# Deformable sampling by whole tiles: VectorE in 12 operations in place of 27, exponentials and sums on ScalarE

## The chip, the cores and the metric

The kernel runs on one core of a Trainium2 chip. The metric is the device time of one execution in microseconds (us). The engines are TensorE (PE in the rows, its weight loads PEld), VectorE (DVE), ScalarE (ACT), GpSimd (POOL) and SyncE (SP), the last of which here only issues DMAs.

## The reference

The program is a stack of layers. The part that matters is layer 0, a deformable attention over 4 images of 64 x 64 pixels with 128 channels in 4 groups of 32. For each pixel and group it takes 9 taps at positions that a small network gives, and each tap is a bilinear mix of 4 corner cells:

```python
out = gather(y0, x0) * (1 - wy_) * (1 - wx_) + gather(y0, x0 + 1) * (1 - wy_) * wx_ + gather(y0 + 1, x0) * wy_ * (1 - wx_) + gather(y0 + 1, x0 + 1) * wy_ * wx_
return out * mask[:, None]
...
attn = jax.nn.softmax(jnp.einsum('bgnc,bgckn->bgnk', qf, ks_), axis=-1)
out = jnp.einsum('bgnk,bgckn->bgnc', attn, vs_)
...
return out @ w_proj + b_proj
```

So every pixel has 36 taps (4 groups of 9), each with 4 corners, of keys and of values; scores against the query, a softmax over the 9 taps of a group, and a weighted sum. Layer 1 is a linear attention over the same tokens; layers 2 and 3 follow it.

## The kernel before

Layers 0 and 1 are one function, `first_layers`. For each image b, `points(b)` computes convolutions, offsets and weights, and writes a table of records (one record holds the 4 corners' keys and values of a cell, 256 floats) and a table `meta` with one row of 308 floats a pixel (36 indices, 144 corner weights, the query). Then the sampling loop goes over 128 tiles of 128 pixels (32 tiles an image). `linear(b)` is layer 1.

The sampling loop is software-pipelined by hand. GpSimd issues 36 indirect DMAs a tile (line 511), one per tap, each of which gathers 128 records of 1 KB into `rec`. `rec` is a ring of 4 half tiles (18 taps each), so two tiles fit. VectorE works a tile in two halves h = 0, 1. A half is: multiply keys by query (L1051), reduce to dots (L1052), weight (L1053), sum corners (L1054), maximum (L1055), subtract (L1056); wait for ScalarE's exponential (L780); sum (L1062), reciprocal (L1063), share (L1064), corner weights (L1066), multiply values (L1068), reduce into `att_t` (L1070). L1049 copies the query into PSUM ahead of a tile. Each of these goes through `Chain`, which makes the next VectorE instruction wait for the semaphore `s_dve` of the one before. `scored(t, h)`, `summed(t, h)` and `added(t)` are values that `s_dve` has reached at these points. GpSimd may gather half h of tile t+2 when `summed(t, h)` is reached.

After a tile TensorE turns `att_t` (L678), ScalarE copies it out of PSUM (`turned`, L769), TensorE projects (`project`, L668), VectorE adds residual and bias (`add`, L1030 and L1031, in the second half of the next tile), and ScalarE stores (`store`, L773).

The work of `points(1..3)` (47 slots each) and `linear(0..2)` (38 slots each) is spread over the same loop: the generator `sides` hands out 2 slots a tile, in the order points 1, points 2, linear 0, points 3, linear 1, linear 2, on every engine at a place of its own in the code. TensorE's side work are "jobs": a group of matmuls into one of 4 PSUM banks `ps`, which ScalarE copies out (L706 for the qkv jobs of `points`, L758 for the qv jobs of `linear`, others alike). Job n waits until the copy of job n-4 is made. ScalarE copies a slot's jobs one slot later (qkv jobs in the same slot). The longest side work of VectorE is the depthwise filter: 24 slots of `points(b)` with 9 operations each (L840, L842).

## Time and profile before

| what | value |
|---|---|
| time, median of 3 runs | 9669.89 us (9655.2 to 9689.33) |
| profiled execution: span | 9686.6 us |
| VectorE busy | 6067.7 us, 8431 instructions |
| GpSimd busy | 4575.1 us, 4608 of its instructions are gathers |
| TensorE busy | 3083.5 us |
| ScalarE busy | 1385.9 us |
| first and last gather start | 216.8 us, 6828.6 us |
| last reduce of the sampling loop ends | 6883 us |

The profiled execution's span, 9686.6 us, is its whole time; it is 0.2% above the median of the runs. Sampling, with the side work beside it, takes the stretch from 217 to 6883 us. The remaining 2804 us are layers that the change doesn't touch.

How to read the times of TensorE: a matmul's row tells when it was issued and an end that is modelled; when its result was there is seen at the engine that waited for it.

### The profile page before, as it was taken

What the parts mean: (1) busy time and instruction counts of PE and PEld (TensorE: products, weight loads), DVE (VectorE), ACT (ScalarE), POOL (GpSimd) and SP (SyncE); (2) the same over time, 40 slices, a digit from 0 to 9 for tenths busy, and PEclk for the clock granted to TensorE, in tenths of its full rate; (3) what the DMA queues carried; (4) which work ended last, traced back from release to release, by engine and by line L of the source; (5) the groups of instructions that cost most, each with busy time, mean ns of one, the idle gap of its engine ahead of it and who ended that gap; (6) DMA issues with size and microseconds to landing.
All of it is one profiled execution on the core that took longest, in us unless ns stands there. A gap on an engine that the chain in (4) does not pass through costs nothing. (4 is left out here: it accounts for less than half of the span.)

```text
span 9686.6 us, 108210 instructions
## 1 busy us (share of the span) xinstructions
PE 3083.5 (32%) x41476; PEld 2213.2 (23%) x41476; DVE 6067.7 (63%) x8431; ACT 1385.9 (14%) x2582; POOL 4575.1 (47%) x4747
## 2 busy tenths in 40 slices
PE   4102101021001101021001100101255476999997
PEld 2001000010001000010001000100233365788885
DVE  6567675776775557685875557545673565555554
ACT  1000000000000000000000000000122232444442
POOL 0766666666677567666777667766100000000000
PEclk7555555565555555555555555555677788999998
DMA  4434345343353234343453234323123443222224
GB/s 86 121 93 111 95 111 145 95 111 92 109 155 99 80 94 126 90 114 91 111 155 99 86 97 121 102 88 96 38 45 127 110 105 90 60 66 67 66 66 179
DMA packets 822930, 966.58 MB, mean 100 GB/s; under 512 B 283028, under 2 KB 643560, under 8 KB 817896
## 3 DMA queue, kind: packets, MB, share of 16 engines
q0 software_dynamic: 221184, 604.27, 21.1%
q1 hardware_dynamic: 573880, 321.25, 13.4%
q10 hardware_dynamic: 27440, 34.87, 1.0%
q8 instruction: 328, 5.37, 0.2%
q14 instruction: 98, 0.80, 0.0%
HBM read 797.64 MB, written 155.99 MB: 98 GB/s over the span
## 5 line engine op out<-in xcount | busy, mean ns | idle before, releaser
L511 POOL DMA_INDIRECT l_rec<-records,l_row x4608 | 4518.7, 981 | 2309.6 <-issue 1421.4
L1070 DVE TENSOR_REDUCE l_att_t<-l_rec 128x64 f32<-128x2304 f32 x256 | 1025.5, 4006 | 8.8
L2323 DVE COPY l3p_mix<-l3p_ps 128x512 f32<-128x512 f32 x1024 | 659.9, 686 | 576.1 <-PE l3p_ps L2199 576.1
L668 PE MATMUL l_pso<-l_wo,l_att_c 128*128 128x128 f32 x256 | 101.9, 501 | 2560.9 <-issue 1684.5
L1051 DVE TENSOR_TENSOR l_rec<-l_rec,l_psv 128x2304 f32<-128x2304 f32 x256 | 653.7, 2553 | 202.5 <-DMA l_rec<-records,l_row 88.7
L678 PE MATMUL l_pso<-l_id,l_att_t 128*128 128x128 f32 x128 | 58.0, 453 | 2114.1 <-DVE l_att_t L1070 1472.7
L1068 DVE TENSOR_TENSOR l_rec<-l_rec,l_psv 128x2304 f32<-128x2304 f32 x256 | 653.7, 2554 | 100.6 <-DVE l_psv L1066 67.8
L780 ACT ACTIVATE l_prob<-l_score 128x18 f32<-128x18 f32 x256 | 56.1, 219 | 4381.0 <-DVE l_score L1056 1442.2
L1052 DVE TENSOR_REDUCE l_psv<-l_rec 128x72 f32<-128x2304 f32 x256 | 655.6, 2561 | 11.4 <-remote 1.7
L668 PEld LDWEIGHTS l_pso<-l_wo,l_att_c 128*128 128x128 f32 x256 | 64.2, 312 | 2607.0 <-issue 1717.9
L2285 ACT ACTIVATE l3p_mix<-l3p_ps 128x512 f32<-128x512 f32 x1024 | 557.7, 597 | 662.8 <-PE l3p_ps L2199 662.8
L2199 PE MATMUL l3p_ps<-l3p_psi,l3p_ms 32*128 32x128 f32 x16384 | 611.6, 283 | 21.3 <-DVE l3p_mix L2323 16.8
L2160 POOL COPY l3p_four<-l3p_fil 128x128 f32 (+1 forms) x64 | 18.8, 294 | 1197.0 <-PE l3p_psm L2252 1196.1
L2199 PEld LDWEIGHTS l3p_ps<-l3p_psi,l3p_ms 32*128 32x128 f32 x16384 | 519.4, 186 | 180.5 <-ACT l3p_mix L2285 108.7
L678 PEld LDWEIGHTS l_pso<-l_id,l_att_t 128*128 128x128 f32 x128 | 23.7, 185 | 2166.6 <-DVE l_att_t L1070 1506.8
L1062 DVE TENSOR_REDUCE l_psv<-l_prob 128x2 f32<-128x18 f32 x256 | 46.0, 180 | 572.0 <-issue 297.7
L842 DVE SCALAR_TENSOR_TENSOR l_psc<-l_area,l_wd,l_psc 128x512 f32<-128x512 f32 x504 | 381.0, 756 | 24.7 <-DVE l_psc L842 6.2
L2149 POOL MEMSET l3p_xs<- 128x4096 f32 x1 | 3.5, 3512 | 800.9 <-POOLq L55 800.9
L1030 DVE TENSOR_TENSOR l_done<-l_pso,l_res 128x128 f32<-128x128 f32 x128 | 37.4, 292 | 485.2 <-remote 354.5
L1514 POOL MEMSET l2b_res<- 128x512 f32 x1 | 0.5, 525 | 595.2 <-POOLq L55 595.2
L2216 PE MATMUL l3p_psy<-l3p_mix,l_mats 128*32 128x128 f32 x8192 | 259.6, 273 | 1.0 <-ACT l3p_yr L2294 0.8
L2216 PE MATMUL l3p_psy<-l3p_mix,l3p_xs 128*32 128x128 f32 x8192 | 258.9, 273 | 0.0
(359 smaller groups left out, 6394.6 us busy)
## 6 DMA issues: line engine op xcount, KB each, us to landing
l_rec<-records,l_row POOLq DMA_INDIRECT x4608
l2b_w<-l_w SPq DMA_DIRECT2D x32, 1024.0 KB, 10.9
records<-l_area SPq DMA_DIRECT2D x48, 512.0 KB
l_row<-meta SPq DMA_DIRECT2D x124, 154.0 KB
l_x_hat<-l3a_xout ACTq DMA_DIRECT2D x32, 512.0 KB, 4.6
l3p_xin<-l_x_hat SPq DMA_DIRECT2D x128, 128.0 KB, 3.1
l_y_raw<-l3p_yr SPq DMA_DIRECT2D x64, 256.0 KB, 3.4
l3p_yin<-l_y_raw SPq DMA_DIRECT2D x128, 128.0 KB, 2.9
```

The source lines that it names most:

```text
L511: pool.indirect_dma_start(out=rec[:, r, k, :], out_offset=None, in_=records[b].rearrange("r c d -> r (c d)"), in_offset=bass.IndirectOffse ...
L668: pe.matmul(ps_p, att_c[:, :], wo0_s[:, :], start=True, stop=True).then_inc(s_proj, 1)
L678: pe.transpose(ps_a, att_t[t % 2][:, :], id_s[:, :]).then_inc(s_att, 1)
L842: step_a(dve.scalar_tensor_tensor(acc if t < TAPS - 1 else to, window(f, g, t), wd_s[:, f, t:t + 1], acc, ALU.mult, ALU.add))
L1051: step(dve.tensor_tensor(keys, keys, asked.broadcast_to([P, HG, TAPS * CORNERS, HC]), ALU.mult))
L1052: step(dve.tensor_reduce(flat, rec[:, r, :, :].rearrange("p k (c d) -> p (k c) d", c=CORNERS)[:, :, 0:HC], AX, ALU.add))
L1068: step(dve.tensor_tensor(values, values, ps_w.rearrange("p (g m) -> p g m", g=HG).unsqueeze(3).broadcast_to([P, HG, TAPS * CORNERS, HC]), ...
L1070: step(dve.tensor_reduce(att_t[two][:, HG * HC * h:HG * HC * (h + 1)].rearrange("p (g d) -> p g d", g=HG), values.rearrange("p g m d -> p ...
L2199: mm = pe.matmul(bank.rearrange("p (x c e) -> p x c e", x=2, e=2)[:, i // 2, :, i % 2], ms[32 * g:32 * g + 32, 4 * q + i, :], psi[s][32 * ...
L2216: mm = pe.matmul(ps_y[32 * g:32 * g + 32, c, :], flat[:, 32 * m - 8 * r:32 * m - 8 * r + 32], mix[s][:, :, 2 * m + kind, :], start=r == 0 ...
L2285: act.activation(mix[t.side(0)][:, x:x + 2, :, :].rearrange("p x c e -> p (x c e)"), ps[(2 * q + h) % 3][:, 0, :], ACT.Copy).then_inc(s_se ...
L2323: dve.tensor_copy(mix[t.side(0)][:, x:x + 2, :, :].rearrange("p x c e -> p (x c e)"), ps[(2 * q + h) % 3][:, 1, :]).then_inc(s_setd, 1)
```

## The change

A tile is worked on whole. `Chain` steps on VectorE go from 27 a tile to 12: the two halves are joined, the query's copy goes to ScalarE (`ask`), the maximum and subtraction become one minimum (the query is now scaled by a negative factor, and ScalarE's exponential takes `scale=-1.0` and the minimum as `bias`), and the sums come from `accum_out` of 4 exponentials, one a group (`weigh`). GpSimd's gathers of tile t+2 now wait once, for all of tile t (`summed(t)`). On TensorE and ScalarE the loop is written in another order.

```diff
-            def half(b, s, h):
-                r = 2 * (s % 2) + h
-                for k in range(HT):
-                    c = HT * h + k
...
+            def gather(b, s):
+                for c in range(GT):
+                    r = 2 * (s % 2) + c // HT
...
-                for h in range(2):
-                    if s >= 2:
-                        pool.wait_ge(s_dve, summed(s - 2, h))
-                    half(0, s, h)
+                if s >= 2:
+                    pool.wait_ge(s_dve, summed(s - 2))
+                gather(0, s)
...
             for t in range(TILES):
-                if t:
-                    project(t - 1)
+                pe.wait_ge(s_dve, summed(t))
+                pe.transpose(ps_a, att_t[t % 2][:, :], id_s[:, :]).then_inc(s_att, 1)
+                project(t)
                 next(side)
                 next(side)
-                pe.wait_ge(s_dve, summed(t, 1))
-                pe.transpose(ps_a, att_t[t % 2][:, :], id_s[:, :]).then_inc(s_att, 1)
-            project(TILES - 1)
...
+            def ask(t):
+                act.wait_ge(s_row[t % AHEAD], 16 * (t // AHEAD + 1))
+                return act.activation(ps_q, row[t % AHEAD][:, QUERY:META], ACT.Copy)
+
+            def weigh(t):
+                act.wait_ge(s_dve, scored(t))
+                for g in range(GROUPS):
+                    k = slice(TAPS * g, TAPS * g + TAPS)
+                    ins = act.activation(prob[:, k], score[:, k], ACT.Exp, bias=low[:, g:g + 1], scale=-1.0, accum_out=total[:, g:g + 1])
+                if t + 1 < TILES:
+                    ins = ask(t + 1)
+                ins.then_inc(s_exp, 1)
...
             for t in range(TILES):
-                for h in range(2):
-                    act.wait_ge(s_dve, scored(t, h))
-                    act.activation(prob[:, :], score[:, :], ACT.Exp).then_inc(s_exp, 1)
-                    if h == 0 and t >= 1:
-                        turned(t - 1)
-                    if h == 0 and t >= 2:
-                        store(t - 2)
-                    next(side)
+                weigh(t)
+                if t >= 1:
+                    store(t - 1)
+                turned(t)
+                next(side)
+                next(side)
...
                 for h in range(2):
-                    r = 2 * two + h
...
+                    dve.wait_ge(s_rec[2 * two + h], 16 * HT * (t // 2 + 1))
+                step(dve.tensor_tensor(keys, keys, asked.broadcast_to([P, GROUPS, TAPS * CORNERS, HC]), ALU.mult))
+                step(dve.tensor_reduce(flat, held.rearrange("p k (c d) -> p (k c) d", c=CORNERS)[:, :, 0:HC], AX, ALU.add))
+                step(dve.tensor_tensor(flat, flat, wgt, ALU.mult))
+                step(dve.tensor_reduce(score[:, :], dots[:, :, :], AX, ALU.add))
+                dve.tensor_reduce(low[:, :], score[:, :].rearrange("p (g k) -> p g k", k=TAPS), AX, ALU.min).then_inc(s_dve, 1)
...
+                if t >= 1:
+                    add(t - 1, step)
...
+                dve.wait_ge(s_exp, t + 1)
+                step(dve.reciprocal(inverse, total[:, :]))
...
-                    next(side)
+                next(side)
+                next(side)
```

ScalarE's order, at the qv jobs of `linear(0)`, before. `l_prob` is the exponential of a half tile, `l_att_c` is `turned`, `x<-l_done` the store, L758 the copies of qv jobs.

```order
L780 ACTIVATE l_prob<-l_score 128x18 [waits l01_dve]
L769 ACTIVATE l_att_c<-l_pso 128x128 [waits l01_att]
L773 DMA x<-l_done 128x128 [waits l01_dve]
L758 ACTIVATE l_area<-l_ps 128x512 [waits l01_l_job] x3
L780 ACTIVATE l_prob<-l_score 128x18 [waits l01_dve]
L758 ACTIVATE l_area<-l_ps 128x512 [waits l01_l_job] x3
```

And the same place after the change:

```order
L772 ACTIVATE l_prob,l_total<-l_score,l_low 128x9 [waits l01_dve]
L772 ACTIVATE l_prob,l_total<-l_score,l_low 128x9 x3
L766 ACTIVATE l_psv<-l_row 128x128 [waits l01_row3]
L783 DMA x<-l_done 128x128 [waits l01_dve]
L779 ACTIVATE l_att_c<-l_pso 128x128 [waits l01_att]
L755 ACTIVATE l_area<-l_ps 128x512 [waits l01_l_job] x6
```

Before, a tile's two exponentials stand 3 copies apart, and its turned result is that of the tile before; now a tile has all its exponentials in one place, and 6 copies and its own `turned` stand between them and the next tile's.

GpSimd's order in the loop before (the wait on `l01_dve` is the one for `summed`):

```order
L511 DMA l_rec<-records,l_row 128x256 [waits l01_dve,l01_row2]
L511 DMA l_rec<-records,l_row 128x256 x17
L511 DMA l_rec<-records,l_row 128x256 [waits l01_dve]
L511 DMA l_rec<-records,l_row 128x256 x17
L511 DMA l_rec<-records,l_row 128x256 [waits l01_dve,l01_row3]
```

And after:

```order
L512 DMA l_rec<-records,l_row 128x256 [waits l01_dve,l01_row2]
L512 DMA l_rec<-records,l_row 128x256 x35
L512 DMA l_rec<-records,l_row 128x256 [waits l01_dve,l01_row3]
L512 DMA l_rec<-records,l_row 128x256 x35
```

The second wait within a tile is gone, and the first now stands for a whole tile.

## Rows read from the trace of the kernel before

**Rows 1.** The page: span; busy us, share, instructions of engines.

```profile
span 9686.6 us, 108210 instructions
PE 3083.5 (32%) x41476; PEld 2213.2 (23%) x41476; DVE 6067.7 (63%) x8431; ACT 1385.9 (14%) x2582; POOL 4575.1 (47%) x4747
```

**Rows 2.** Stretches: us, busy PE, PEld, DVE, ACT, POOL; clock, DMA share, GB/s.

```profile
217.00:6883.00 6666.00, 843.29 (x2254) 470.72 (x2254) 4365.83 (x4755) 349.65 (x812) 4518.46 (x4608) 0.53 0.38 107
217.00:1487.00 1270.00, 175.94 (x382) 78.02 (x382) 868.56 (x933) 61.28 (x149) 883.29 (x904) 0.53 0.39 109
...
2696.00:3696.00 1000.00, 109.86 (x369) 80.45 (x369) 595.36 (x661) 54.80 (x122) 682.94 (x684) 0.53 0.37 106
3696.00:4917.00 1221.00, 174.19 (x385) 78.33 (x385) 870.03 (x937) 61.31 (x150) 826.54 (x860) 0.53 0.38 107
...
5911.00:6883.00 972.00, 108.90 (x370) 80.22 (x370) 595.93 (x661) 55.58 (x122) 640.53 (x642) 0.52 0.34 98
```

**Rows 3.** Line 511, the gathers: what ended the idle time before them.

```profile
L511 POOL DMA_INDIRECT l_rec<-records,l_row x4608: 943/949/5119, 216.8 to 6828.6; - x192
...
  DVE l_att_t L1070: 552.1, 74
...
  DVE l_psv L1049: 119.0, 7
```

**Rows 4.** VectorE's groups from 217 to 6883 us: busy, mean ns | idle before.

```profile
L1070 DVE TENSOR_REDUCE l_att_t<-l_rec 128x64 f32<-128x2304 f32 x256 | 1025.5, 4006 | 8.8
L1052 DVE TENSOR_REDUCE l_psv<-l_rec 128x72 f32<-128x2304 f32 x256 | 655.6, 2561 | 11.4 <-remote 1.7 <-issue 0.9
L1068 DVE TENSOR_TENSOR l_rec<-l_rec,l_psv 128x2304 f32<-128x2304 f32 x256 | 653.7, 2554 | 100.6 <-DVE l_psv L1066 67.8 <-issue 22.2 <-remote 5.6
L1051 DVE TENSOR_TENSOR l_rec<-l_rec,l_psv 128x2304 f32<-128x2304 f32 x256 | 653.7, 2553 | 202.5 <-DMA l_rec<-records,l_row 88.7 <-remote 42.6 <-issue 42.6
...
L1049 DVE COPY l_psv<-l_row 128x128 f32<-128x128 f32 x127 | 37.4, 294 | 46.9 <-remote 20.4 <-DVE l_area L842 14.0 <-issue 7.2
```

**Rows 5.** The sum over six stretches with filter slots, 36 tiles in all.

```profile
sum 1917.00, PE 270.27 PEld 131.38 DVE 1469.95 ACT 76.95 POOL 1283.24; mean PE 45.05 PEld 21.90 DVE 244.99 ACT 12.82 POOL 213.87
```

**Rows 6.** Timeline in a filter stretch: start, us, instruction [idle before].

```profile
634.27 0.18 DVE L1063 RECIPROCAL l_psv<-l_psv 128x2 f32<-128x2 f32 x1 [2.30 <-remote]
...
636.38 0.18 DVE L1064 TENSOR_TENSOR l_psv<-l_prob,l_psv 128x18 f32<-128x18 f32 x1 [1.93 <-remote]
...
638.48 2.55 DVE L1068 TENSOR_TENSOR l_rec<-l_rec,l_psv 128x2304 f32<-128x2304 f32 x1 [1.16 <-DVE l_psv L1066]
```

**Rows 7.** Timeline at the qv jobs of `linear(0)`, with gathers running.

```profile
3040.05 0.60 ACT L758 ACTIVATE l_area<-l_ps 128x512 f32<-128x512 f32 x1 [14.73 <-remote]
...
3040.70 2.08 PE L643 MATMUL l_ps<-l_wn,l_area 128*128 128x256 f32 x4 [11.50 <-issue]
...
3051.25 0.60 ACT L758 ACTIVATE l_area<-l_ps 128x512 f32<-128x512 f32 x1 [10.60 <-remote]
...
3062.45 0.60 ACT L758 ACTIVATE l_area<-l_ps 128x512 f32<-128x512 f32 x1 [10.60 <-remote]
3062.95 0.21 ACT L780 ACTIVATE l_prob<-l_score 128x18 f32<-128x18 f32 x1
3063.26 0.18 DVE L1062 TENSOR_REDUCE l_psv<-l_prob 128x2 f32<-128x18 f32 x1 [15.25 <-issue]
```

**Rows 8.** Timeline at the qkv jobs of `points(2)`: gathers stop, jobs go on.

```profile
1707.68 0.69 ACT L706 ACTIVATE l_area<-l_ps,l_bn 128x512 f32<-128x512 f32 x1 [4.21 <-issue]
...
1712.58 0.69 ACT L706 ACTIVATE l_area<-l_ps,l_bn 128x512 f32<-128x512 f32 x1 [4.21 <-remote]
...
1715.39 1.85 ACT L706 ACTIVATE l_area<-l_ps,l_bn 128x512 f32<-128x512 f32 x3
...
1723.89 0.95 POOL L511 DMA_INDIRECT l_rec<-records,l_row  x1 [15.54 <-DVE l_psv L1049]
```

**Rows 9.** Line 739, an exponential with `accum_out`: ns min/median/max.

```profile
L739 ACT ACTIVATION_READ_ACCUMULATOR l_area<-l_area,l_kmax x4: 187/188/188, 2984.3 to 6932.8; 128x1 f32 x4
```

More of the change, by code:

```diff
@@ L284, in first_layers @@
         s_gate = st.gates()
-        STEPS, ADDS = 27, 2
+        STEPS, ADDS = 12, 2
         TILES = BATCH * NT
@@ L292, in cells_of, with begun, scored, summed @@
             return records[b][0:GROUPS * TH * TH, :, :].rearrange("(g y x) c d -> g y x c d", g=GROUPS, x=TH)
-        def begun(t, h):
-            return STEPS * t - ADDS * int(t >= 1) + 13 * h
-        def scored(t, h):
-            return begun(t, h) + 6 + int(h == 0)
+        def begun(t):
+            return STEPS * t - ADDS * int(t >= 1)
+        def scored(t):
+            return begun(t) + 5
         def added(t):
-            return scored(t + 1, 1) + ADDS if t + 1 < TILES else begun(TILES, 0) + ADDS
-        def summed(t, h):
-            return begun(t, h) + 12 + (1 if h == 0 else ADDS * int(t >= 1))
+            return (scored(t + 1) if t + 1 < TILES else begun(TILES)) + ADDS
+        def summed(t):
+            return begun(t + 1)
         PG, LG = 47, 38
@@ L526, in _ @@
                         hold(pool, s_row[s], 16 * i + 16, s_gate[1])
-                        for h in range(2):
-                            hold(pool, s_dve, AHEAD * STEPS * (i - 1) + summed(s + 2, h), s_gate[1])
-                            half(b, s, h)
+                        hold(pool, s_dve, AHEAD * STEPS * (i - 1) + summed(s + 2), s_gate[1])
+                        gather(b, s)
         @block.tensor
@@ L715, in points @@
                                 for t in range(AHEAD):
-                                    act.activation(row[t][:, QUERY:META], bank[:, t * P:t * P + P], ACT.Copy, scale=float(HC) ** -0.5)
+                                    act.activation(row[t][:, QUERY:META], bank[:, t * P:t * P + P], ACT.Copy, scale=-float(HC) ** -0.5)
                             if at == 0 and b in (1, 2):
@@ L776, in _ @@
             side = sides(points, linear)
+            ask(0).then_inc(s_asked, 1)
             for t in range(TILES):
-                for h in range(2):
-                    act.wait_ge(s_dve, scored(t, h))
-                    act.activation(prob[:, :], score[:, :], ACT.Exp).then_inc(s_exp, 1)
-                    if h == 0 and t >= 1:
-                        turned(t - 1)
-                    if h == 0 and t >= 2:
-                        store(t - 2)
-                    next(side)
-            turned(TILES - 1)
-            store(TILES - 2)
+                weigh(t)
[4 more added lines that the diff above has]
+                next(side)
             store(TILES - 1)
@@ L1074, in _ @@
-            step = Chain(dve, s_dve, s_gate[2], begun(TILES, 0))
+                step = Chain(dve, s_dve, s_gate[2], begun(t))
+                held = rec[:, 2 * two:2 * two + 2, :, :].rearrange("p r k d -> p (r k) d")
+                view = held.rearrange("p (g k) (c d) -> p g (k c) d", k=TAPS, c=CORNERS)
+                asked = ps_q.rearrange("p (g o d) -> p g o d", o=1, d=HC)
+                keys, values = view[:, :, :, 0:HC], view[:, :, :, HC:2 * HC]
+                wgt = row[s][:, GT:QUERY]
@@ new lines, in _ @@
+                step(dve.tensor_reduce(score[:, :], dots[:, :, :], AX, ALU.add))
+                dve.tensor_reduce(low[:, :], score[:, :].rearrange("p (g k) -> p g k", k=TAPS), AX, ALU.min).then_inc(s_dve, 1)
+                step.n += 1
+                assert step.base + step.n == scored(t)
+                if t >= 1:
+                    add(t - 1, step)
+                    assert step.base + step.n == added(t - 1)
+                dve.wait_ge(s_exp, t + 1)
+                step(dve.reciprocal(inverse, total[:, :]))
@@ new lines, in _ @@
+                step(dve.tensor_tensor(share.rearrange("p (g k) -> p g k", k=TAPS), prob[:, :].rearrange("p (g k) -> p g k", k=TAPS),
+                                       inverse.unsqueeze(2).broadcast_to([P, GROUPS, TAPS]), ALU.mult))
+                step(dve.tensor_tensor(ps_w.rearrange("p (k c) -> p k c", c=CORNERS), wgt.rearrange("p (k c) -> p k c", c=CORNERS),
+                                       share.unsqueeze(2).broadcast_to([P, GT, CORNERS]), ALU.mult))
+                step(dve.tensor_tensor(values, values, ps_w.rearrange("p (g m) -> p g m", g=GROUPS).unsqueeze(3).broadcast_to(
+                    [P, GROUPS, TAPS * CORNERS, HC]), ALU.mult))
@@ L1075, in _ @@
+                dve.tensor_reduce(att_t[two][:, :].rearrange("p (g d) -> p g d", g=GROUPS),
+                                  values.rearrange("p g m d -> p g d m"), AX, ALU.add).then_inc(s_dve, 1)
+                step.n += 1
+                assert step.base + step.n == summed(t)
+                next(side)
+                next(side)
+            step = Chain(dve, s_dve, s_gate[2], begun(TILES))
             add(TILES - 1, step)
```

66 lines of the change are left out of this document (19 added, 47 removed).

## The prediction

> **What bounds the kernel now.** I read the stretches first. Sampling with its side work lasts from 217 to 6883 us, 6666 us of the span of 9686.6 us; of this VectorE is busy 4366 us and GpSimd 4518 us [rows 1, 2]. Neither is full, so I looked for who waits for whom. The gathers come next: 4608 of them, 36 a tile, start between 216.8 and 6828.6 us; a gather takes 0.95 us and 0.30 us lie between two, so a tile costs 36 x 1.25 = 45.1 us of issue, and 128 tiles 5773 us. The waits of GpSimd for VectorE's last reduce and for its next copy are 552.1 + 119.0 = 671 us in 81 waits [rows 3]. So GpSimd is the bound for 5773 us, and about 850 us are lost to waits and slower gathers. By parts: the three stretches of `points` take 1209 to 1270 us for 23.5 tiles each (52 us a tile), the three of `linear` 972 to 1000 us for 19 tiles (52 us) [rows 2]. VectorE hardly ever waits for data: 88.7 us in all before L1051 [rows 4].
>
> What holds VectorE up is of two kinds. In filter slots its small steps cost far more than their work: 0.18 us of work stands behind gaps of 2.30, 1.93 and 1.16 us [rows 6]; six such stretches, 36 tiles, take 1917 us with 1470 us of VectorE work, 53 us a tile [rows 5]. Elsewhere TensorE's side jobs are slow: while gathers run, ScalarE's copies of qv jobs come 11.2 us apart though one job is 4 matmul and 4 weight-load instructions, 1.4 us each, and the exponential behind them in ScalarE's order comes as late as they: VectorE's sum stood idle 15.25 us for it [rows 7]. When GpSimd stands still (15.54 us), the jobs soon go fast: copies at 1707.68 and 1712.58 are 4.9 us apart, then three come within 1.85 us [rows 8]. The whole kernel thus has a self-regulating loop: gathers slow TensorE, TensorE delays the exponentials, these delay VectorE, and VectorE in the end stops the gathers.
>
> **What the change saves on VectorE.** The four large operations of a half are 4.01 + 2.56 + 2.55 + 2.55 = 11.67 us, 23.35 us a tile [rows 4]. By the copy of 128 elements in 0.294 us and the multiply of 2304 in 2.554 us, an element costs 1.04 ns and an instruction 0.16 us more, so joining two halves saves 4 x 0.16 = 0.65 us. Of 19 small operations of 0.17 to 0.29 us, about 4.0 us, 8 stay with about 2.1 us. With 0.035 us between instructions a tile goes from 28.4 to 25.2 us: 3.2 us x 128 = 410 us of VectorE time, which counts only where VectorE is last. In filter slots the exposed small steps fall from about 19 to 8, so I halve the gaps: busy 25.2 + 14.4 for two filter slots (18 operations of 0.76 us and their gaps) + 10 of gaps = 49 us against 53.
>
> The Trainium skill speaks for the change here: "VectorE: DVE Perf Modes", section on the TRN2 errata, says that an instruction on SBUF data pays a fixed latency, so that one large tile pays once and many small ones each time; its fp32 formula has 151 cycles at 0.96 GHz, by which 15 instructions fewer save an estimated 302 us in all. The rows' 0.16 us agree with it.
>
> **What it adds on ScalarE.** Four exponentials at 0.21 us, each with an accumulator read of 0.19 us [rows 7, 9], and the query's copy, 0.29 us by VectorE's copy [rows 4]: 1.9 us between `scored` and the release of VectorE, in place of two times 0.21 + 0.1. The copy was off VectorE's wait before; this is +1.3 us in VectorE's line a tile, about what the copy and the two sums saved.
>
> **What it takes away in slack.** Before, half h of tile t+2 needs half h of tile t: the buffer comes free half by half, three halves' issue after it was filled (3 x 22.6 = 67.7 us), and needs about 2 us of landing and 14 us of work: some 51 us in which VectorE may be held up before GpSimd stops. Now it must be free one tile's issue, 45.1 us, after it was filled, and needs 2 + 25 us: 18 us of slack. A hold of 40 us that GpSimd rode out before now stops it for about 20.
>
> **What it puts in VectorE's line.** This is the term that decides. After the change ScalarE's order is exponentials(t), store, turned(t), two slots of copies, exponentials(t+1), and TensorE's is turn(t), project(t), two slots of jobs. Call x the end of tile t on VectorE. TensorE starts the jobs of two slots only after turn and project, 6 instructions of 1.4 us = 8.4 us; ScalarE must copy the first slot's jobs before it gives the next exponentials. For qv, kt, vt, qt jobs that is 3 x 11.2 = 33.6 us; then 1.9 us, then the second part of VectorE's tile, 2.55 x 2 + 4.01 x 2 + three small ones = 13.7 us. Next x: 8.4 + 33.6 + 1.9 + 13.7 = **57.6 us** later. Before, the exponential of the second half stood between the two slots, and the transposes came a tile later against the side work; such tiles cost 75 us when they came in a row but VectorE and GpSimd had worked ahead, and the average over `linear` was 52.
>
> Jobs that need more than GpSimd's 45.1 us: in the qkv slots ScalarE copies all 12 jobs (12 x 5.6 = 67 us; one such job is 4 instructions), in the off4/offm slots 3 jobs of 12 instructions (50 us), in the last slots of `linear` 3 qt jobs and 2 of 16 instructions (78 us). GpSimd then stops at x + 45.1, the jobs stay slow some 5 us more [rows 8], then run fast, some 2 us: x + 52 + 1.9 + 13.7 = **68 us**.
>
> **The sum.** In one `points` of 23.5 tiles I count, by slots: 3 tiles of qkv and 3 of off4/offm at 68, 3 of offc/offs at 65, 1.5 of qt and 2 of kt/vt at 58, 6 filter tiles without jobs at 49, 5 others at 46: 408 + 195 + 203 + 294 + 230 = 1330 us, against (1270 + 1209 + 1221)/3 = 1233 with the first tile's 65 us of filling in the first one; without it 1212. That is about +118. In one `linear` of 19 tiles: 3 at 68, 8.5 at 58, 7.5 at 46: 204 + 493 + 345 = 1042, against 989 on the mean (994 is the middle one): +53. Three of each: 3 x (118 + 53) = 513; the first tile, of which VectorE now needs both halves, +7. Some tiles that I count at 68 overlap slots at a fraction, and a fast tile follows where VectorE is ahead; I take 70 us off for this: **+450 us**, 10137 us in the profile's terms and 10120 against the median, which is 0.2% lower.
>
> **Rivals.** (a) *TensorE gets quicker, the faster side* (0.20): if its instruction under gathers costs r = 0.9 in place of 1.4 us, for instance because 15 fewer semaphore steps a tile on VectorE relieve what both share, a 58 us tile is 30r + 15.6 = 43, so 46 by GpSimd (36 tiles, -432); offc/offs and off4/offm tiles come to 50 and 53 (18 tiles, -270), qkv and the last slots of `linear` to 64 and 65 (18 tiles, -63). That is -765 on the forecast, 9360 us; by a straight line between the two it breaks even at r = 1.1. For it: the jobs are fast as soon as GpSimd stands. Against it: they are slow because of the gathers, and these stay. (b) *It cancels* (0.05): the saving in filter tiles, 36 x 4 to 36 x 8 = 150 to 290 us, against loaded tiles that keep their fast followers: 9640 to 9700. (c) *The handshakes too* (0.20): in slots 3 to 5 of `points` and 7 to 9, 24, 25 of `linear` VectorE waits for TensorE's job of the same slots. Before, that job had been issued most of a tile earlier; now it starts with VectorE's slot, behind 8.4 us of turn and project. 33 such waits of 8 to 12 us with 18 us of slack: +150 to +300 on the forecast, 10300 to 10450. (d) The forecast (0.55): 9800 to 10300.
>
> The granted clock, 0.52 to 0.54 in the stretches [rows 2], is near the lower level of 1.2 GHz before and should be so after; I give it nothing.
>
> **Numbers.** A measurement can tell about 0.3%, 29 us. Slower by more: 0.55 + 0.20 = 0.75; same 0.05; faster 0.20. The range leaves 1 in 10 of the faster end and 1 in 10 of the slowest: 9620 to 10480.
>
> **What would show it.** Right: the gathers' waits for VectorE's last reduce grow from 671 to about 1100 us, in most tiles; VectorE's idle time moves to the reciprocal behind the exponentials, with ScalarE copying late jobs; copies still 11.2 and 5.6 us apart while gathers run; VectorE's work falls by about 400 us; filter tiles near 49 us. Wrong: copies of jobs much closer together under gathers (then rival a), or small steps on VectorE with no gaps, or exponentials that do not stand behind late copies.

## The result, and the profile after

The changed kernel takes 9843.85 us (median of 4 runs, 9839.98 to 9855.23), the kernel before, run beside it, 9679.61 (4 runs, 9655.2 to 9691.68): ratio 1.0169, interval 1.0153 to 1.0185, 164 us slower. The forecast was +450 with the range 9620 to 10480: the sign and the range held, the size was nearly three times too large.

The page of the changed kernel, to be read against [rows 1]:

```profile
span 9853.4 us, 106326 instructions
PE 3062.5 (31%) x41476; PEld 2212.3 (22%) x41476; DVE 5717.2 (58%) x6511; ACT 1524.3 (15%) x3478; POOL 4639.8 (47%) x4747
```

VectorE works 350 us less and GpSimd, with the same 4608 gathers, 65 us more. The stretches between the ends of the same tiles as in [rows 2], with the same columns:

```profile
217.00:1478.00 1261.00, 165.36 (x382) 74.73 (x382) 801.80 (x573) 87.56 (x316) 883.25 (x891) 0.54 0.39 108
1478.00:2711.00 1233.00, 172.06 (x377) 75.16 (x376) 778.16 (x564) 85.71 (x307) 828.01 (x838) 0.53 0.40 109
2711.00:3745.00 1034.00, 103.65 (x373) 78.30 (x373) 534.56 (x373) 76.15 (x257) 688.95 (x684) 0.52 0.37 103
3745.00:4960.00 1215.00, 167.24 (x385) 75.93 (x385) 811.21 (x578) 87.72 (x317) 845.29 (x855) 0.54 0.39 107
4960.00:6004.00 1044.00, 102.28 (x369) 75.53 (x368) 545.02 (x375) 76.10 (x256) 690.79 (x687) 0.52 0.37 104
6004.00:7034.00 1030.00, 99.86 (x369) 74.49 (x369) 544.71 (x376) 75.45 (x254) 647.36 (x656) 0.53 0.32 93
```

The three `points` stretches took 1270 + 1209 + 1221 = 3700 us and now take 3709. The three of `linear` took 2966 and now take 3108. So 142 of the 151 us by which sampling ends later lie in `linear`. The other 16 us of the longer span lie behind the loop (2819 in place of 2804 us), where the instructions are the same; the kernels of the experiments take 2794 to 2823 us there, and nothing here tells why.

Line 512, the gathers, as [rows 3]:

```profile
L512 POOL DMA_INDIRECT l_rec<-records,l_row x4608: 940/946/5072, 217.3 to 6968.4; - x192
...
  DVE l_att_t L1074: 744.8, 39
...
  DVE l_rec L1056: 1019.9, 77
```

GpSimd waits for VectorE 744.8 us in 39 places (before 671 in 81): fewer and longer, but only 74 us more. The row below it tells of VectorE waiting 1019.9 us for gathers; the same view of the kernel before has 107.7 us. VectorE's groups from 217 to 7034 us (busy, mean ns | idle before), as [rows 4]:

```profile
L1056 DVE TENSOR_TENSOR l_rec<-l_rec,l_psv 128x4608 f32<-128x4608 f32 x128 | 634.0, 4953 | 1044.7 <-DMA l_rec<-records,l_row 892.4 <-issue 129.6 <-remote 19.2
L1037 DVE TENSOR_TENSOR l_done<-l_pso,l_res 128x128 f32<-128x128 f32 x127 | 37.0, 291 | 92.3 <-issue 55.7 <-remote 36.6
L1057 DVE TENSOR_REDUCE l_psv<-l_rec 128x144 f32<-128x4608 f32 x128 | 635.0, 4961 | 4.4
L1067 DVE RECIPROCAL l_psv<-l_total 128x4 f32<-128x4 f32 x128 | 23.8, 186 | 802.9 <-issue 693.9 <-ACT l_psv L766 108.2 <-ACT l_prob L772 0.8
L1068 DVE TENSOR_TENSOR l_psv<-l_prob,l_psv 128x36 f32<-128x36 f32 x128 | 25.5, 200 | 4.5
L1070 DVE TENSOR_TENSOR l_psv<-l_row,l_psv 128x144 f32<-128x144 f32 x128 | 39.8, 311 | 4.4
L1072 DVE TENSOR_TENSOR l_rec<-l_rec,l_psv 128x4608 f32<-128x4608 f32 x128 | 634.0, 4953 | 6.0 <-issue 1.6
L1074 DVE TENSOR_REDUCE l_att_t<-l_rec 128x128 f32<-128x4608 f32 x128 | 1004.2, 7845 | 4.4
```

and the groups of before that answer to these (217 to 6883 us):

```profile
L1030 DVE TENSOR_TENSOR l_done<-l_pso,l_res 128x128 f32<-128x128 f32 x127 | 37.1, 292 | 483.4 <-remote 354.5 <-PE l_pso L668 68.9 <-issue 52.8
L1062 DVE TENSOR_REDUCE l_psv<-l_prob 128x2 f32<-128x18 f32 x256 | 46.0, 180 | 572.0 <-issue 297.7 <-ACT l_prob L780 196.1 <-DVE l_score L1056 33.7
L1063 DVE RECIPROCAL l_psv<-l_psv 128x2 f32<-128x2 f32 x256 | 45.7, 179 | 131.9 <-remote 57.7 <-DVE l_psv L1062 37.4 <-issue 31.0
L1064 DVE TENSOR_TENSOR l_psv<-l_prob,l_psv 128x18 f32<-128x18 f32 x256 | 46.5, 181 | 130.7 <-DVE l_psv L1063 53.7 <-remote 42.8 <-issue 28.5
L1066 DVE TENSOR_TENSOR l_psv<-l_row,l_psv 128x72 f32<-128x72 f32 x256 | 60.8, 238 | 95.2 <-DVE l_psv L1064 73.8 <-issue 12.0 <-remote 3.8
```

Read in pairs: the small steps stood idle for 131.9 + 130.7 + 95.2 = 358 us, now (L1068, L1070) 8.9; the wait for the projected tile fell from 483.4 to 92.3. Against this, the wait for exponentials rose from 572.0 to 802.9, and that for data from 202.5 to 1044.7. The change gave VectorE some 350 us of work and more than 700 us of stalls back, and all of it was turned into waiting for others, and more: VectorE's idle time in the loop rose from 2300 to 2802 us. In a filter stretch (as [rows 6]) this looks so:

```profile
612.83 0.19 DVE L1067 RECIPROCAL l_psv<-l_total 128x4 f32<-128x4 f32 x1 [0.94 <-ACT l_psv L766]
613.05 0.20 DVE L1068 TENSOR_TENSOR l_psv<-l_prob,l_psv 128x36 f32<-128x36 f32 x1
613.28 0.31 DVE L1070 TENSOR_TENSOR l_psv<-l_row,l_psv 128x144 f32<-128x144 f32 x1
...
645.30 4.95 DVE L1056 TENSOR_TENSOR l_rec<-l_rec,l_psv 128x4608 f32<-128x4608 f32 x1 [4.61 <-DMA l_rec<-records,l_row]
```

No gap is left between small steps, and VectorE, done early, waits for the gathers. The same 36 filter tiles as in [rows 5], again as a sum over six stretches (420, 420, 415, 214, 197 and 215 us):

```profile
sum 1881.00, PE 230.13 PEld 120.21 DVE 1351.34 ACT 112.39 POOL 1336.56; mean PE 38.35 PEld 20.03 DVE 225.22 ACT 18.73 POOL 222.76
```

These stretches hold two kinds of tiles that went opposite ways. Three tiles with filter work and no jobs, first before (188 us, 63 a tile), then after (125 us, under 42 a tile), with the columns of [rows 2]:

```profile
551.00:739.00 188.00, 3.90 (x10) 2.14 (x10) 123.76 (x137) 1.81 (x9) 120.83 (x121) 0.50 0.30 89
546.00:671.00 125.00, 3.81 (x9) 2.04 (x9) 114.74 (x90) 5.07 (x30) 94.94 (x96) 0.50 0.36 106
```

The last tile of the first stretch, in which TensorE has its jobs, took 50 us (896 to 946) and now takes 102 (823 to 925). A loaded tile of `linear(0)` (as [rows 7]), with the turned copy of the tile ahead of it:

```profile
3088.22 0.28 ACT L779 ACTIVATE l_att_c<-l_pso 128x128 f32<-128x128 f32 x1 [18.61 <-remote]
...
3143.03 0.48 PE L673 MATMUL l_pso<-l_id,l_att_t 128*128 128x128 f32 x1 [24.09 <-DVE l_att_t L1074]
...
3163.82 0.28 ACT L779 ACTIVATE l_att_c<-l_pso 128x128 f32<-128x128 f32 x1 [34.51 <-remote]
3163.99 1.57 ACT L755 ACTIVATE l_area<-l_ps 128x512 f32<-128x512 f32 x3
...
3180.62 0.60 ACT L755 ACTIVATE l_area<-l_ps 128x512 f32<-128x512 f32 x1 [15.05 <-remote]
...
3191.82 0.60 ACT L755 ACTIVATE l_area<-l_ps 128x512 f32<-128x512 f32 x1 [10.60 <-remote]
...
3203.02 0.60 ACT L755 ACTIVATE l_area<-l_ps 128x512 f32<-128x512 f32 x1 [10.61 <-remote]
...
3204.94 0.18 DVE L1067 RECIPROCAL l_psv<-l_total 128x4 f32<-128x4 f32 x1 [33.50 <-issue]
```

This is the loop that the prediction drew, with its copies 11.2 us apart and the reciprocal behind them. The three copies made at once are those of the slot ahead of the turn, for which the forecast charged nothing either. What it did not draw: the turned tile came 20.8 us after the turn. That fits a TensorE that still has that slot's jobs to work off before the turn: from one turned copy to the next (3088.22 to 3163.82) are 75.6 us, and TensorE has 54 instructions in between (2 of the turn, 4 of the projection, 48 of six jobs), 1.40 us each. The kernel before has the same 75.6 us for 54 instructions in `linear(1)`. So in a row of such tiles TensorE's own line sets the length, before and after the change.

The side work of VectorE waits for TensorE too. In slot 24 of each `linear` VectorE stands for TensorE's context product (128 instructions in slots 21 to 24):

```profile
3451.17 0.16 DVE L988 RECIPROCAL l_ksum<-l_ksum 128x1 f32<-128x1 f32 x1 [78.78 <-remote]
5650.26 0.16 DVE L988 RECIPROCAL l_ksum<-l_ksum 128x1 f32<-128x1 f32 x1 [77.22 <-remote]
6679.77 0.16 DVE L988 RECIPROCAL l_ksum<-l_ksum 128x1 f32<-128x1 f32 x1 [77.07 <-remote]
```

The kernel before stood here once, 54.2 us. In slot 18 of `linear` three waits of 33 to 38 us are new (109 us in all), before the statistics of L810 there are 67 us in place of 16, and in slots 31 and 32 of `points` VectorE waits 225 us for the offs jobs in place of 115, 48.4 and 47.0 us of it in two places:

```profile
1092.13 0.49 DVE L863 TENSOR_TENSOR l_area<-l_ps,l_bo 128x324 f32<-128x324 f32 x1 [48.44 <-issue]
```

Together these waits are some 635 us in the loop, before 185.

### The profile page after: what moved, and what is told of

It is laid out like the page before. It is cut to its first block and busy times, and to the rows that moved or that the text cites. A ratio compares the mean times of both kernels' runs of the same rounds, so it can differ in the third digit from the quotient of the medians.

```text
span 9853.4 us, 106326 instructions
## 1 busy us (share of the span) xinstructions
PE 3062.5 (31%) x41476; PEld 2212.3 (22%) x41476; DVE 5717.2 (58%) x6511; ACT 1524.3 (15%) x3478; POOL 4639.8 (47%) x4747
## 5 line engine op out<-in xcount | busy, mean ns | idle before, releaser
L512 POOL DMA_INDIRECT l_rec<-records,l_row x4608 | 4583.7, 995 | 2384.4 <-issue 1423.6
L1056 DVE TENSOR_TENSOR l_rec<-l_rec,l_psv 128x4608 f32<-128x4608 f32 x128 | 634.0, 4953 | 1044.7 <-DMA l_rec<-records,l_row 892.4
L1074 DVE TENSOR_REDUCE l_att_t<-l_rec 128x128 f32<-128x4608 f32 x128 | 1004.2, 7845 | 4.4
L1057 DVE TENSOR_REDUCE l_psv<-l_rec 128x144 f32<-128x4608 f32 x128 | 635.0, 4961 | 4.4
L1072 DVE TENSOR_TENSOR l_rec<-l_rec,l_psv 128x4608 f32<-128x4608 f32 x128 | 634.0, 4953 | 6.0 <-issue 1.6
L772 ACT ACTIVATE l_prob<-l_score,l_low 128x9 f32<-128x9 f32 x512 | 147.6, 290 | 2219.8 <-DVE l_low L1060 873.4
L1067 DVE RECIPROCAL l_psv<-l_total 128x4 f32<-128x4 f32 x128 | 23.8, 186 | 802.9 <-issue 693.9
L779 ACT ACTIVATE l_att_c<-l_pso 128x128 f32<-128x128 f32 x128 | 35.5, 277 | 2459.3 <-issue 868.5
L579 PE MATMUL l_ps<-l_area,l_wp 96*32 96x512 f32 (+1 forms) x384 | 218.1, 732 | 102.1 <-issue 59.9
```

Source lines behind the costliest of these rows:

```text
L512: pool.indirect_dma_start(out=rec[:, r, c % HT, :], out_offset=None, in_=records[b].rearrange("r c d -> r (c d)"), in_offset=bass.Indirect ...
L579: last = pe.matmul(bank[0:m, :], wp_s[:, dy, o:o + m], pads[0][0:3 * HC, 8 * at + dy:8 * at + dy + 8, 0:W], start=dy == 0, stop=dy == 2)
L772: ins = act.activation(prob[:, k], score[:, k], ACT.Exp, bias=low[:, g:g + 1], scale=-1.0, accum_out=total[:, g:g + 1])
L1056: step(dve.tensor_tensor(keys, keys, asked.broadcast_to([P, GROUPS, TAPS * CORNERS, HC]), ALU.mult))
L1057: step(dve.tensor_reduce(flat, held.rearrange("p k (c d) -> p (k c) d", c=CORNERS)[:, :, 0:HC], AX, ALU.add))
L1072: step(dve.tensor_tensor(values, values, ps_w.rearrange("p (g m) -> p g m", g=GROUPS).unsqueeze(3).broadcast_to([P, GROUPS, TAPS * CORNERS ...
```

## The experiments

They came in six sets, each with the kernel before beside it on the same chip. In two sets the kernel before took 8855 to 8860 us in place of 9680 to 9700, and this has to be known to read the rest.

**Where the kernel before takes 8860 us.** Three parts of the change, one at a time: the loop order of TensorE and ScalarE, GpSimd's wait once a tile, ScalarE's sums.

> The kernel before with one part of the change alone: TensorE and ScalarE in the changed loop order (turn and project a tile, then two slots of jobs; both exponentials of a tile, store, turned, then two slots of copies), VectorE's side slots both at the end of a tile. Halves, 27 steps and the hand-back of buffers by halves stay. Theory O (the order costs: the next tile's exponentials stand behind two slots of late copies): 9830 to 10000 us, 150 to 320 over before. Theory S (the lost slack of the hand-back by whole tiles costs, the order is harmless as long as buffers come free by halves): within 50 us of before, 9640 to 9730.

> The kernel before with one edit: GpSimd waits once a tile, for all of tile t, before it gathers tile t+2. Theory O: the order of before hides most of it, +20 to +80 us, 9700 to 9760. Theory S: +150 us or more, 9830 or above, since this alone is then the loss of the change.

> The kernel before with its halves, its loop order and its hand-back, but ScalarE forms the exponentials with their sums and copies the query (22 steps a tile in place of 27). Both theories: VectorE's work falls by some 128 x (0.29 + 2 x 0.21 + 2 x 0.18) = 137 us. If the small steps' gaps cost as the prediction said (about 1.1 us each beside its work in filter tiles), 5 fewer of them in 36 filter tiles give 200 us, and the sum is 9400 to 9550. If small steps only cost where VectorE is last, 9580 to 9680.

Measured: 8869.25, 8855.85 and 8857.23 us, ratios 1.0008, 0.9996 and 0.9995 with intervals of 0.001 to either side. No expectation fits, since the floor itself had moved. Of the first of them the gathers' line:

```profile
L511 POOL DMA_INDIRECT l_rec<-records,l_row x4608: 942/946/5172, 218.2 to 6032.4; - x192
```

VectorE's reciprocal among its groups, to be read against L1063 above:

```profile
L1059 DVE RECIPROCAL l_psv<-l_psv 128x2 f32<-128x2 f32 x255 | 45.6, 179 | 8.8
```

and ScalarE's copies of qv jobs in its timeline, to be read against [rows 7]:

```profile
2734.44 0.60 ACT L756 ACTIVATE l_area<-l_ps 128x512 f32<-128x512 f32 x1 [1.12 <-PE l_ps L643]
2736.15 0.60 ACT L756 ACTIVATE l_area<-l_ps 128x512 f32<-128x512 f32 x1 [1.11 <-PE l_ps L643]
```

The gathers run 5814 us without a stop, 1.262 us each; small steps have no gaps (8.8 us in 255), and the qv copies are 1.7 us apart in place of 11.2. The granted clock over the loop is 0.54 here too. So the slow TensorE and the slow small steps under gathers are not always there, and where they are not, GpSimd alone is the bound and each of these parts moves the time by 0.1% or less. A later set fell into the same condition, on a chip (number 9) that had shown 9686 us in an earlier set:

> The changed kernel with TensorE's context product of linear (128 TensorE instructions) in slots 20 to 23 in place of 21 to 24; VectorE still takes its result in slot 24, where it stood 79, 78 and 77 us for it. Theory H (handshakes: VectorE waits in the slot in which TensorE has just begun, and that is the loss in linear): most of 3 x 78 us of waiting goes, 120 to 200 us off, 9660 to 9750. Theory B (TensorE is last there anyway, and VectorE waits for something else of TensorE's soon after): under 60 us off, 9800 or more.

> The kernel before with the same move of the context product by one slot. It waited 54 us in one place for it and under 3 us in the two others. Theory H: 0 to 50 us off. Theory B: within 20 us.

> Whole tiles on VectorE with all the remedies at once: TensorE's and ScalarE's order of before, a side slot of VectorE between its minimum and its wait for the exponentials, values in two halves with hand-back by halves, context product one slot earlier. From 9735 (order and side slot) 74 for the halves and 50 to 150 for the context product if they add: 9510 to 9610, below the kernel before. If the waits only move from one place to another: 9650 to 9720.

> Before's halves and order with ScalarE's sums and query copy (22 steps), and the context product one slot earlier. Theory H: 9620 to 9665, the sum of the two small gains. Theory B: 9650 to 9690.

Measured: ratios 1.0022, 0.9995, 1.0017, 1.0003, so none of these expectations was put to its test. The two with whole tiles are 18 and 17 us slower. The gathers run 5819 and 5816 us from first to last, against 5813 and 5814 in the two with halves; the last tile is worked whole only when its last gather has landed, and its last reduce ends 33 us after the last gather in place of 17.

**The change again, and its loop order undone.**

> The changed kernel, unaltered. In the three runs before this one the kernel before took 8860 us in place of 9670: gathers 1.26 us apart without a stop (4608 in 5815 us), and ScalarE found a job's result 0.4 to 1.1 us after its last matmul in place of 5 to 30 us. Theory P (the change costs only where TensorE's results come late under the gathers; the rest is hidden by GpSimd): where the kernel before takes about 8860 us, the changed one takes 8840 to 8890 us, ratio 0.998 to 1.003; where it takes about 9670, 9820 to 9860, ratio 1.017. Rival H (handshakes and the lost slack cost in any state): over 8950 us where before takes 8860.

Measured: 9869.31 against 9699.86, ratio 1.0179 (1.0159 to 1.0198); the tiles end 5 us (the first) to 26 us (the last) later than in the first trace, whose span is 29 us shorter. The ratio is theory P's, 1.017, for this condition. The handshake rival's number for 8860 could not be tested with this very kernel; the version above, which moves the context product besides, gave +18 us where it asked for +90.

The loop order undone. Besides what is shown, VectorE adds tile t-1 after its last reduce of tile t, no longer ahead of the exponentials, and the turn waits for it because both use the same PSUM bank; so this is not the order alone:

```diff
             for t in range(TILES):
-                pe.wait_ge(s_dve, summed(t))
-                pe.transpose(ps_a, att_t[t % 2][:, :], id_s[:, :]).then_inc(s_att, 1)
-                project(t)
+                if t:
+                    project(t - 1)
                 next(side)
                 next(side)
+                pe.wait_ge(s_dve, added(t - 1) if t else summed(t))
+                pe.transpose(ps_a, att_t[t % 2][:, :], id_s[:, :]).then_inc(s_att, 1)
...
-                turned(t)
+                if t >= 1:
+                    turned(t - 1)
+                if t >= 2:
+                    store(t - 2)
                 next(side)
                 next(side)
```

> The changed kernel with TensorE's and ScalarE's loop order of before: project(t-1), two slots of jobs, then turn tile t; exponentials(t), turned(t-1), store(t-2), two slots of copies. VectorE adds tile t-1 after its last reduce of tile t, and the turn waits for it. Where the kernel before takes about 8860 us: theory P no difference (8840 to 8890), since GpSimd's issue alone bounds the loop. Where it takes about 9670: theory O (the order costs) 9500 to 9700, theory S (the lost slack costs) 9800 to 9880.

Measured: 9817.23, ratio 1.0129 (1.0106 to 1.0152): 52 us back. The time lies in theory S's range, though S said that the order gives nothing back. VectorE's wait for exponentials fell to 574 us, but its `add` now waited 595 us for the projection.

**The parts one at a time on the kernel before, where it takes 9686.**

The order: TensorE's loop as in the change, VectorE's two side slots at the end of a tile, and on ScalarE

```diff
                     act.activation(prob[:, :], score[:, :], ACT.Exp).then_inc(s_exp, 1)
-                    if h == 0 and t >= 1:
-                        turned(t - 1)
-                    if h == 0 and t >= 2:
-                        store(t - 2)
-                    next(side)
+                if t >= 1:
+                    store(t - 1)
+                turned(t)
+                next(side)
+                next(side)
```

The hand-back:

```diff
-                        for h in range(2):
-                            hold(pool, s_dve, AHEAD * STEPS * (i - 1) + summed(s + 2, h), s_gate[1])
+                        hold(pool, s_dve, AHEAD * STEPS * (i - 1) + summed(s + 2, 1), s_gate[1])
+                        for h in range(2):
                             half(b, s, h)
```

> The same kernel as the first of these experiments (before, with the changed loop order on TensorE and ScalarE and VectorE's two side slots at the end of a tile), again, to see it where the kernel before takes about 9690 us. The reverse edit on the changed kernel gave 52 us back. Theory O (the order is a third of the loss): 9720 to 9790, 30 to 100 over before. Theory O2 (the order is most of it when halves stay): over 9830. If the kernel before takes about 8860 us, no difference.

> Before with GpSimd's wait once a tile, again, where the kernel before takes about 9690 us. Theory S (lost slack is most of the loss): +90 to +200 us, 9780 to 9890. Theory O: under +50.

> Before with ScalarE's sums and query copy, 22 steps in place of 27, again, where the kernel before takes about 9690 us. If each small step under the gathers costs 1 to 2 us: -100 to -300 us, 9400 to 9590. If VectorE's steps are not what ends last: within 50 us of before.

Measured: order 9869.94, ratio 1.0181 (1.0161 to 1.0201), as theory O2 said; hand-back 9726.62, 1.0037 (1.0024 to 1.0050), as O said; sums on ScalarE 9665.19, 0.9978 (0.9960 to 0.9997), within 50 us, as the second expectation said. The loop order (with VectorE's side slots at the tile's end) costs on half tiles what the whole change costs; undone on whole tiles it gave back 52 us, so the parts do not add. The groups of the version with the order (L1058 takes the exponentials, L1026 the projection):

```profile
L1058 DVE TENSOR_REDUCE l_psv<-l_prob 128x2 f32<-128x18 f32 x256 | 46.1, 180 | 969.4 <-ACT l_prob L778 628.7 <-issue 276.5 <-DVE l_score L1052 33.1
...
L1026 DVE TENSOR_TENSOR l_done<-l_pso,l_res 128x128 f32<-128x128 f32 x127 | 37.1, 292 | 5.3 <-issue 0.7 <-DVE l_score L1052 0.4
```

and what ended the idle time before its context product's line, L977:

```profile
  remote: 177.3, 3
```

The wait for the projection (483.4 us) is gone; that for exponentials went from 572.0 to 969.4 and that for the context product from 54.2 to 177.3. With ScalarE's sums GpSimd's waits for VectorE fell to 489.3 us, but its gathers took 4612 us in place of 4519: of 182 us less waiting 93 came back as longer gathers, and the gain is 21 us.

**Hand-back by halves on the changed kernel.** The values are multiplied and reduced in two halves, and GpSimd waits for each half.

```diff
+                for h in range(2):
+                    g2 = slice(HG * h, HG * h + HG)
+                    held_w = ps_w[:, HT * CORNERS * h:HT * CORNERS * (h + 1)]
+                    step(dve.tensor_tensor(values[:, g2], values[:, g2], held_w.rearrange("p (g m) -> p g m", g=HG).unsqueeze(3).broadcast_to(
+                        [P, HG, TAPS * CORNERS, HC]), ALU.mult))
+                    ins = dve.tensor_reduce(att_t[two][:, HG * HC * h:HG * HC * (h + 1)].rearrange("p (g d) -> p g d", g=HG),
+                                            values[:, g2].rearrange("p g m d -> p g d m"), AX, ALU.add)
```

> The changed kernel, but VectorE multiplies and reduces the values in two halves, and GpSimd may fill a half as soon as it is reduced: 14 steps a tile, the first half comes free 6.6 us before the second. Theory S: each of the 41 waits of GpSimd for the last reduce (18.6 us on the mean) gets up to 6 us shorter, 41 x 6 = 250 us less wait, of which the half that VectorE then waits for data is not won: 9650 to 9780 where before takes 9690. Theory O: 9820 to 9880, since what is late is the tile's end.

Measured: 9785.32, ratio 1.0096 (1.0076 to 1.0116), 84 us below the changed kernel of the other set (80 by the two ratios), 5 us above theory S's range and 35 below O's. GpSimd's waits fall from 762.4 to 624.4 us, by 138 where 250 were expected: the 6.6 us count.

**Half of the qv matmuls left out**, in the changed kernel and in the one before.

```diff
                         if kind == "qv":
-                            for t in range(2):
+                            for t in range(1):
```

> The changed kernel with half of the matmuls of linear's 48 qv jobs left out (the second image tile's q and v of each job are then stale): 4 of a job's 8 TensorE instructions fewer, nothing else. Theory T (where the kernel before takes about 9690 us, TensorE's instructions at 1.4 us each set the length of these tiles): 48 x 4 x 1.4 = 269 us of TensorE, of which 150 to 270 come off: 9580 to 9710. Rival W (the loss is from handshakes and waits around the tile's end, not from TensorE's rate): under 80 us come off, 9780 or more. Where the kernel before takes about 8860 us: no difference.

> The kernel before with the same half of the qv matmuls left out (again the second image tile's q and v of each job are stale). Theory T: the order of before lets TensorE work ahead, so less comes off than in the changed kernel, 80 to 200 us: 9490 to 9610. Rival W: under 50 us.

Measured: 9808.94, ratio 1.0133 (1.0113 to 1.0153), about 45 us off by the ratios (60 by the times of the two sets), as rival W said; and 9628.28, ratio 0.9944 (0.9925 to 0.9964), 53 us off, between the two ranges and close to W. Theory T falls for the total, but the copies say something else (changed kernel, one tile):

```profile
3135.52 1.57 ACT L755 ACTIVATE l_area<-l_ps 128x512 f32<-128x512 f32 x3
3137.36 0.60 ACT L755 ACTIVATE l_area<-l_ps 128x512 f32<-128x512 f32 x1 [0.27 <-issue]
3138.21 0.60 ACT L755 ACTIVATE l_area<-l_ps 128x512 f32<-128x512 f32 x1 [0.26 <-issue]
3139.07 0.60 ACT L755 ACTIVATE l_area<-l_ps 128x512 f32<-128x512 f32 x1 [0.26 <-PE l_ps L642]
```

With 4 instructions fewer in each job the copies do not come 5.6 us apart, but at once. A tile now has 24 TensorE instructions of jobs and 6 of turn and project; with 48 and 6 the last three copies were 15.7, 11.2 and 11.2 us apart. At 1.4 us each, 30 instructions are 42 us, less than the 50 us that this tile takes, and TensorE is not behind; 54 are 75.6 us, and in the full kernel's tile TensorE is behind from start to end. A first crowded tile still has a head start: the turned copy at 3088.22, the first behind 54 instructions, came only 4.9 us after its reduce, the next one 20.8 us. So the pace of 1.4 us costs nothing as long as TensorE has fewer instructions than the time of the tiles holds, and for all of them in a row of tiles that have more. The qv tiles of `linear(0)` took 65 us less, of the 90 that 16 jobs with 4 instructions fewer are worth at 1.4 us, and 47 us of it was lost again by slot 26, where VectorE's waits for the context product had grown (298 us in three places, in place of 233).

**A side slot between minimum and exponentials.** On top of the loop order undone:

```diff
+                next(side)
                 dve.wait_ge(s_exp, t + 1)
                 step(dve.reciprocal(inverse, total[:, :]))
```

with one `next(side)` fewer at the tile's end.

> The changed kernel with the loop order of before on TensorE and ScalarE (as in the experiment with that order), and VectorE's first side slot of a tile put between its minimum and its wait for the exponentials. VectorE stood 574 us for the exponentials and 595 us for the project in the version without this. If side work can fill these waits: 80 to 200 us off 9817, 9620 to 9740 where before takes 9690. If the copies are late whatever VectorE does meanwhile: within 40 us of 9817.

Measured: 9734.75, ratio 1.0057 (1.0037 to 1.0076), 82 us off the version without it in another set (70 by the ratios): the small end of the first expectation. Work that is put in front of a wait hides part of it.

**The context product one slot earlier, and all remedies at once.**

```diff
-                    if 21 <= slot < 25:
-                        if slot == 21:
+                    if 20 <= slot < 24:
+                        if slot == 20:
```

> The changed kernel with the context product in slots 20 to 23, again, where the kernel before takes about 9690 us. Theory H (the handshake in slot 24 is the loss in linear): 120 to 200 us off 9869, 9660 to 9750. Theory B (TensorE is last there anyway): under 60 us off, 9800 or more.

> All remedies at once on whole tiles, again, where the kernel before takes about 9690 us: 9510 to 9610 if they add; 9650 to 9720 if the waits only move from one place to another.

Measured: 9822.88, ratio 1.0145 (1.0125 to 1.0165), 46 us off (33 by the ratios, where the two intervals allow some 27 of noise), within theory B's number. The rows tell more (VectorE's wait in slot 24):

```profile
3417.43 0.16 DVE L988 RECIPROCAL l_ksum<-l_ksum 128x1 f32<-128x1 f32 x1 [43.06 <-remote]
5632.27 0.16 DVE L988 RECIPROCAL l_ksum<-l_ksum 128x1 f32<-128x1 f32 x1 [77.39 <-remote]
6661.50 0.16 DVE L988 RECIPROCAL l_ksum<-l_ksum 128x1 f32<-128x1 f32 x1 [77.42 <-remote]
```

`linear(0)` begins at an even slot (94), so slots 23 and 24 lie in different tiles and the wait shrank by 36 us; that tile took 24 us less than in both traces of the changed kernel. `linear(1)` and `linear(2)` begin at odd slots (179, 217): 23 and 24 lie in the same tile, and nothing changed. Two thirds of the wait came back as time, and only the move across a tile's border shortened it. All remedies at once: 9647.24, ratio 0.9964 (0.9945 to 0.9984), 34 us faster than before and 222 below the changed kernel (208 by the ratios); 37 us short of the first expectation and 3 us below the second one's range. Of the kernels that do all the work it is the fastest where the kernel before takes 9680, by a third of a per cent, and 0.17% slower than it where that takes 8855.

## Why the prediction was right in sign and wrong in size

**What bounds the kernel: right**, for the condition that its trace shows.

**VectorE's saving: right.** Forecast 3.2 us a tile; busy time fell by (4366 - 4015)/128 = 2.7, and 15 spaces of 0.035 us are 0.5 more. The four large operations fell from 2988.5 [rows 4] to 634.0 + 635.0 + 634.0 + 1004.2 = 2907.2 us: 81.3 us for 512 instructions fewer, 0.159 us each. The Trainium skill's fixed latency per instruction ("VectorE: DVE Perf Modes", section on the TRN2 errata; 151 cycles at 0.96 GHz are an estimated 0.157 us) agrees with that.

**Small steps: mis-sized.** The gaps were to be halved ("so I halve the gaps", with no row for it), which made a filter tile without jobs 49 us in place of 53. They vanished, and such tiles went from 63 to under 42 us. The 53 was a mean over stretches that also hold tiles with jobs; that mean fell to 52, since the gain in one kind was used up by the other.

**ScalarE's term: right.** From the minimum's end (611.35) to the reciprocal (612.83) 1.5 us, forecast 1.9.

**Slack: right in kind.** The wait once a tile costs 41 us on the kernel before; halves give 84 back on the changed one.

**The order in VectorE's line: right in kind.** On half tiles the order gives ratio 1.0181 by itself, the whole change 1.0169 to 1.0179. Hand-back (+41), fewer steps (-21) and what the joined halves do, which no run shows by itself, come to about nothing on top. On whole tiles undoing it gave back 52 us, and 134 with a side slot put before the wait.

**The step that failed is "The sum".** It priced each tile by itself, tiles with jobs at 58 to 68 us and filter tiles at 49, and took 70 us off for the tiles that follow fast. By parts: `points` +118 each, measured +9 for all three (1261, 1233, 1215 against 1270, 1209, 1221); `linear` +53 each, measured +47 (142 for three). The small number in `points` is not a small effect but two that cancel. Counted from tile end to tile end in both traces, the 42 tiles of the three `points` in which TensorE has jobs (more than 11 instructions from turn to turn) went from 2166 to 2432 us, +266, and the 28 without from 1468 to 1198, -271; the first tile adds 13. In the forecast's terms: 12.5 tiles with jobs at 64.5 us on the mean, measured 57.9; 11 others at 47.6, measured 42.8. Together that is about 120 us too much in each `points`.

Single tiles look different again. Of those 42 tiles 26 pass at 33 to 51 us, in part below GpSimd's 45.1, and 13 take 72 to 106, more than the 68 that was forecast as the most: what TensorE is behind with is carried into the next tiles, and so is what GpSimd has gathered ahead. The tile of `linear(0)` above takes 75.6 us against 57.6: 20.8 for the turn and 39.2 for projection and three copies where the forecast had 8.4 + 33.6 for all, since it let TensorE begin a tile with nothing left over. That the three `linear` come out right (57.4 us on the mean for 41 tiles with jobs, 47.2 for the others) hides single tiles of 26 to 107 us; that part of the agreement is luck.

**The gathers' waits** were to grow from 671 to 1100 us; they grew to 745, and another 65 us went into slower gathers (995 ns on the mean against 981), a form of loss that the prediction did not have.

**Rival (c), handshakes:** 33 waits of 8 to 12 us were named, for slots 3 to 5 of `points` and 7 to 9, 24 and 25 of `linear`. The mechanism was real and larger than that: VectorE's side work waits some 635 us for TensorE in place of 185. The large ones are few, three of 78 us in slot 24, three of 33 to 38 in slot 18 and two of 47 to 48 in slot 31 of `points`, so most stood in other places than named; waits of 9 to 11 us for offs jobs were there before the change too. **Rival (b)** had the saving of the filter tiles at 150 to 290 us, and 271 is what the tiles without jobs gained; but the tiles with jobs did not keep their fast followers. **Rival (a)** was wrong here, as the pace of late copies did not change. Where the kernel before takes 8860 us TensorE is quick, but there the kernels with whole tiles are 0.2% slower, not faster.

Why whole sets of executions run at 8860 us stays open; no run here varies its cause. The changed kernel as it stands was not run there. That TensorE is late with 54 instructions in a tile and not with 30 is shown in the qv tiles of `linear`; how large its head start can be, and what sets the pace of 1.4 us, is not.

## What to carry to other kernels

When one engine's work falls, list for each of its waits who releases it and whether that one became faster too; here 350 us of work and several hundred of stalls turned into waiting for exponentials, data and TensorE's side results. The order in which the other engines' loops are written was worth as much as the whole change on half tiles: start side work before, not behind, the wait for the tile's end, and put work between a request and the wait for its answer. Count an engine's instructions over a row of tiles, not tile by tile, since it carries what it is behind with. Look at handshakes by the border at which both engines change tile: the move within a tile removed nothing here. And look at kinds of tiles, not at totals: a sum near zero was +266 and -271.

## What the runs showed of the hardware

The same kernel takes 9680 or 8860 us, with the runs of a set within 0.5% in either condition, and one chip showed both at different times. In the first, under indirect gathers, ScalarE stands 10.6 to 15.1 us for one job of TensorE after another, many small VectorE steps of the kernel before start 0.7, 1.4 or 2.1 us apart where each works 0.18 us, and 307 of its gathers (563 of the changed kernel's) take about 1.10 in place of 0.95 us. In the second the jobs are 1.7 us apart, no such step starts more than 0.3 us after the one before it, and 17 gathers take 1.10 us, at nearly the same granted clock (0.54 against 0.53 over the loop). Before a change of some per cent is judged, the kernel before has to be timed beside it, and a difference in one condition may be almost none in the other: 1.0179 here against at most 1.0022 for the kernels with whole tiles.
